# A two-layer sequence kernel: six steps take other places in their engines' queues, and nine of 128 scans run in two halves

## The reference, cut to what matters

```python
# layer 0, per batch
xn = layernorm(x) * (1 + scale) + shift            # from the condition c
x_in, z = split(xn @ in_proj_w.T)                  # 512 channels each
u = silu(causal_conv4(x_in) + conv_b)
dt_r, B, C = split(u @ x_proj_w.T)                 # 64, 16, 16 columns ("x_dbl")
dt = softplus(dt_r @ dt_proj_w.T + dt_proj_b)
# over the 256 positions, for every channel and each of 16 states:
h = h * exp(dt * A) + (dt * u) * B
y = sum over states of h * C
y = (y + u * D_param) * silu(z)
x = x + gate * (y @ out_proj_w.T)
# layer 1, per batch
q, k, v = three linear maps of layernorm(x); softmax of q over 32 features, of k over positions
y = q @ (k.T @ v); x = x + silu(layernorm(y) * (1 + s) + t) @ W_out + b_out
```

## Time and profile before

| what | value |
|---|---|
| median of three runs | 557.86 us (556.59 to 559.77) |
| the profiled execution's own time | 559.76 us |
| span of its profile | 558.0 us |
| mean granted TensorE clock | 0.887 of full speed |
| DVE scans (L1000) | 128, 291.9 us together |
| DVE multiplications by C (L1012) | 96, 117.5 us together |
| ACT decays (L766) | 512 activations, 212.7 us together |

### The profile page before, as it was taken

How to read it: one execution, slowest core, us unless ns; L and a number is a source line. 1 busy time by engine, 2 the same in 40 slices (tenths; PEclk the granted TensorE clock), 3 DMA queues, 4 the chain that set the end, 5 groups by cost and what they waited for, 6 DMA issues and landing times. The chain is left out here.

```text
span 558.0 us, 7398 instructions
## 1 busy us (share of the span) xinstructions
PE 438.2 (79%) x2438; PEld 364.5 (65%) x2438; DVE 504.7 (90%) x520; ACT 430.8 (77%) x992; POOL 449.6 (81%) x306
## 2 busy tenths in 40 slices
PE   8968756769688788779788678769677878959797
PEld 7657445557576677657676667658565766847675
DVE  2489899999999989999999999999999988999853
ACT  2694868689879989798979989799877797686444
POOL 4059979989997989979997999979997979995121
PEclk8978868887899698998899899989899697779899
DMA  8295043102330144011430044003320044000001
GB/s 250 90 330 150 0 140 97 68 23 77 120 114 2 28 153 170 3 28 52 152 122 0 29 156 168 0 11 117 122 85 9 2 165 159 1 0 20 1 1 38
DMA packets 22366, 45.38 MB, mean 81 GB/s; under 512 B 3684, under 2 KB 13556, under 8 KB 22328
## 3 DMA queue, kind: packets, MB, share of 16 engines
q1 hardware_dynamic: 22328, 44.92, 24.6%
HBM read 42.52 MB, written 2.39 MB: 80 GB/s over the span
## 5 line engine op out<-in xcount | busy, mean ns | idle before, releaser
L545 POOL TENSOR_TENSOR hs<-dtu,Br 128x1024 f32<-128x1024 f32 x127 | 296.8, 2360 | 7.9 <-DMA Br<-bc_rows 6.9
L766 ACT ACTIVATE ring<-dt,Aneg 128x256 f32<-128x256 f32 x512 | 212.7, 464 | 44.0 <-DVE hs L1012 39.1
L1000 DVE TENSOR_TENSOR_SCAN ring<-ring,hs 128x1024 f32<-128x1024 f32 x97 | 221.6, 2284 | 10.9 <-ACT ring L766 10.9
L1370 PE MATMUL sums<-ident,hs 128*128 128x128 f32 x1024 | 154.9, 309 | 49.4 <-DVE hs L1012 49.3
L1370 PEld LDWEIGHTS sums<-ident,hs 128*128 128x128 f32 x1024 | 138.6, 162 | 60.6 <-DVE hs L1012 57.5
L1012 DVE TENSOR_TENSOR hs<-ring,Cr 128x1024 f32<-128x1024 f32 x96 | 117.5, 1224 | 3.3
L554 POOL TENSOR_TENSOR hs<-hs,Cr 128x1024 f32<-128x1024 f32 x31 | 73.0, 2356 | 38.7 <-DVE hs L1000 38.7
L1000 DVE TENSOR_TENSOR_SCAN hs<-ring,hs 128x1024 f32<-128x1024 f32 x31 | 70.3, 2268 | 0.0
L1437 PE MATMUL PY<-wqkvo,xT 128*128 128x256 f32 x168 | 48.3, 439 | 0.0
L1437 PEld LDWEIGHTS PY<-wqkvo,xT 128*128 128x128 f32 x168 | 39.6, 236 | 7.7
L1363 PE MATMUL sums<-ident,uD 128*128 128x128 f32 x64 | 14.3, 310 | 32.3 <-DVE ygT L1019 32.3
(11 more groups left out here) (232 smaller groups left out, 681.7 us busy)
## 6 DMA issues: line engine op xcount, KB each, us to landing
Br<-bc_rows SPq DMA_DIRECT2D x32, 512.0 KB, 5.3
Cr<-bc_rows SPq DMA_DIRECT2D x32, 512.0 KB, 4.0
xg<-in_x SPq DMA_DIRECT2D x8, 256.0 KB, 3.0
out<-fin SPq DMA_DIRECT2D x7, 256.0 KB, 4.3
hs<-in_ada_wT SPq DMA_DIRECT2D x3, 512.0 KB, 5.1
win<-in_in_wT SPq DMA_DIRECT2D x2, 512.0 KB, 6.9
hs<-in_W_emb SPq DMA_DIRECT2D x2, 512.0 KB
gate<-gate_rows SPq DMA_DIRECT2D x8, 128.0 KB, 3.1
```

Source lines behind the costliest of these rows:

```text
L545: nc.gpsimd.tensor_tensor(hs[:, g % DBUF], dtu[:, b % 2, dc, :].unsqueeze(1).to_broadcast([P, NQ, T]), Br[:, NQ * q:NQ * q + NQ, :], ALU.m ...
L766: ins = nc.scalar.activation(ring[:, g % 2, j, :], dt[:, b % 2, dc, :], ACT.Exp, scale=Aneg[:, c:c + 1])
L1000: V.tensor_tensor_scan(driven if by_pool(g) else decays, decays, driven, 0.0, ALU.mult, ALU.add).then_inc(s_scan_done, 1)
L1370: ins = M(YT[:, c, :], hs[:, g % DBUF, j, P * c:P * c + P], ident[:, :], is_transpose=True, start=False, stop=(q == UPC - 1 and j == NQ - ...
```

## The change

Two things change.

First, the order. On ACT `copy_xdbl` goes from place 10 to 8, `softplus_parts_0` from 11 to 10 (behind `norm1`, ahead of `finish`), `softplus_parts_1` from 13 to 12. `norm1` stays in place 10. On PE `x_proj` goes from place 7 to 6 and `dt_proj_0` from 8 to 7. The lines with -6 and -5 keep the first half of dt of batch 0, which is made before the first unit, in its old turn.

Second, the scans of unit 0 and of place 8 of each batch (9 units) are done as two scans of 512 elements, two states each. The first waits for two of ACT's four decays, the second for all four. The multiplication by C stays whole, and is done by DVE in these units as before.

```diff
+def in_halves(g):
+    return g == 0 or g % U == 8
+
+def halves_until(g):
+    return sum(in_halves(i) for i in range(g + 1))
...
+        s_da_half = sem("da_half")
...
                     ins = nc.scalar.activation(ring[:, g % 2, j, :], dt[:, b % 2, dc, :], ACT.Exp,
                                                scale=Aneg[:, c:c + 1])
+                    if j == 1 and in_halves(g):
+                        ins.then_inc(s_da_half, 1)
...
-                                   (-11, copy_z), (-6, copy_xdbl), (-5, softplus_parts_0), (-3, softplus_parts_1),
-                                   (19, copy_yg), (25, normalize1), (26, norm1), (30, exp_q), (30, exp_k), (31, mask_v), (32, copy_qT),
+                                   (-11, copy_z), (-8, copy_xdbl), (26, norm1), (-6, softplus_parts_0), (-4, softplus_parts_1),
+                                   (19, copy_yg), (25, normalize1), (30, exp_q), (30, exp_k), (31, mask_v), (32, copy_qT),
...
+                    if step is softplus_parts_0 and g in (-6, -5):
+                        b = 0 if g == -5 else None
...
-                dve.wait_ge(s_da_ready, g + 1)
+                if in_halves(g):
+                    dve.wait_ge(s_da_half, halves_until(g))
+                else:
+                    dve.wait_ge(s_da_ready, g + 1)
...
+                if in_halves(g):
+                    first, second = (slice(0, 2), slice(2, NQ))
+                    for half in (first, second):
+                        if half is second:
+                            dve.wait_ge(s_da_ready, g + 1)
+                        a_half, x_half = (t[:, half].rearrange("p n t -> p (n t)") for t in (ring[:, g % 2], hs[:, g % DBUF]))
+                        ins = V.tensor_tensor_scan(a_half, a_half, x_half, 0.0, ALU.mult, ALU.add)
+                    ins.then_inc(s_scan_done, 1)
+                    dve.wait_ge(s_scan_done, g + 1)
+                    dve.wait_ge(c_loaded[q], 16 * (b + 1))
+                    V.tensor_tensor(hs[:, g % DBUF], ring[:, g % 2], Cr[:, NQ * q:NQ * q + NQ, :], ALU.mult).then_inc(s_hc_dve, 1)
+                    return
...
-                                   (-13, in_proj_3), (39, output), (-9, x_proj), (-8, dt_proj_0), (-6, dt_proj_1),
+                                   (-13, in_proj_3), (-10, x_proj), (39, output), (-9, dt_proj_0), (-6, dt_proj_1),
```

## The result

| | before | after |
|---|---|---|
| median of four runs | 557.25 us (556.59 to 559.77) | 567.95 us (567.66 to 570.46) |
| the profiled execution's own time, span | 559.76, 558.0 us | 567.85, 566.1 us |

A forecast was written before the change was run, and what follows sets the result against it. DVE was taken to set the pace, waiting 10.9 us for ACT's decays. The terms -3.72 + 0.8 + 4.97 + 4.4 = +6.45 us, put on the median 557.86, gave 564.3 us, range 559.5 to 569.5.

The forecast's parts named there:

- The halves at place 8: Place 8: split scans shorten DVE's waits for decays in batches 0 and 2 to 6, -3.72 us; eight splits cost +0.8.
- Unit 0: Start of batch 0: the split gains nothing, since scan 4 stays at about 51.0 behind the load of x.
- Softplus ahead of decays 11: Place 11: ACT's chain becomes 7.39 us against DVE's 5.85; new waits 8.76, old 3.79 gone, +4.97 us.
- The wait for `x_proj`: Between decays 8 and 9, batches 1 to 6: ACT's copy waits for PE, partly at low clock, +4.4 us.
- `softplus_parts_1` at place 12 costs nothing: DVE has `max_qk`: Place 12: the moved step costs 0, as DVE has `max_qk` and two scans before it asks for decays 13.
- rival C: PE's clock stays down as long as before: +12 us, 569.8 us, chance 0.14.
- the two terms of the order: Softplus ahead of decays 11 at place 11, +4.97 us, and ACT's wait for `x_proj` behind decays 8, +4.4.
- Rival A: PE's clock is up at `x_proj` in all batches: +2.65 us, 560.5 us, chance 0.17.
- B: The new order removes the waits at place 11 altogether: -6.7 us, 551.2 us, chance 0.05.
- D: The order does nothing, softplus displacing only ACT's idle time; only the halves count: -2.9 us, 555.0 us, chance 0.04.

The follow-up runs named there:

- e2: The kernel before with the nine split scans and nothing moved: 557.73 us, 1.000 times before.
- e6: The changed kernel with 28 small matmuls, read by nothing, in PE's queue at place 5: 564.05 us, 1.010 times before.
- e1: The changed kernel with no scan in halves, only the six steps moved: 569.55 us, 1.023 times before.
- e3: The changed kernel with both softplus steps back in places 11 and 13, behind decays 11 and 13: 558.69 us, 1.003 times before.
- e7: e3 with 28 small matmuls, read by nothing, in PE's queue at place 5: 553.74 us, 0.991 times before.
- e5: The changed kernel with the second softplus step alone back in place 13: 566.42 us, 1.017 times before.
- e11: e7 with all scans whole: 558.46 us, 1.000 times before.
- e10: e2 with 28 small matmuls in PE's queue at place 5: 552.70 us, 0.992 times before.
- e12: e7 with the layer's bias work on DVE behind unit 7 instead of unit 8: 557.11 us, 0.997 times before.

## Why the prediction was right, and where it was off

**The halves at place 8.** Right in kind: -0.79 in batch 0 and -0.66 in five batches, against -0.84 and -0.575. The split costs 0.04 to 0.05 us and not 0.1: the two halves together take 2.33 to 2.35 us, the whole scan 2.30 where it follows a wait. The 148 ns from the earlier trace rows are in the busy times (2 x 1214 - 2284 = 144), but the second half begins inside the first one's end. The Trainium skill ("VectorE: DVE Perf Modes", the section on the TRN2 errata) counts about 150 cycles at 0.96 GHz for each instruction, by which an instruction more is an estimated 0.156 us; the 0.144 us agrees in busy time, and isn't what the path pays. What was wrong is that the gain goes into the sum whole. In the old order it came back at place 11 in batches 2 and 6 (e2). In the new one it counts whole where `x_proj` is in time, since the wait there is then ACT's own work behind DVE (1.44 us in e6, 1.43 in e1 with whole scans). Where `x_proj` is late, part of it came back: 0.30, 0.54 and 0.36 us in batches 3, 4 and 6.

**Unit 0.** The trace has scan 4 0.70 us earlier, the prediction had none. But the start moves by itself: scan 4 stands at 51.27 in e1, 50.43 in e3, 51.03 in e7 and 48.14 in e2, of which e3, e7 and e2 have the split. Over all traces scan 4 stands at 50.9 to 51.3 where unit 0 is whole and at 48.1 to 51.7 where it is split. Whether the split of unit 0 is worth anything wasn't isolated.

**Softplus ahead of decays 11.** The largest term held: 7.39 us against 5.85, a wait of 1.54. In batch 4 of the changed kernel the chain took 7.52 (323.42 to 330.94), and the wait is 1.44 in e6 where nothing else disturbs. The prediction had 8.76 us of new waits from it; e5 against e3 gives 7.7 on the chip, net of what e3 lost at the taps.

**The wait for `x_proj`.** +4.4 was forecast. In the profiled run places 9 to 11 added 8.31; six chains as in e6 (5 x 1.44 + 0.95 = 8.15) less the old 3.79 are 4.36 of it, so 3.95 fell to this. By batch it was not where I put it. The forecast had 1.2, 1.4, 0.2, 0.1, 0.1 and 1.4 us in batches 1 to 6; over e6's wait stand 0.2, 0.5, 0.3, 0.5, 1.6 (places 9 to 11) and 0.4, and the rest are stops too short for the list. That the sums agree is luck. Batches 4 and 5, which I had as safe, had `x_proj` at 2.70 and 3.17 us, and batches 1 and 6, which I had as slow, at 1.89. Taking the kept clock as the test, e6 is 3.9 us under the changed kernel's median. In e6 PE was busy for 3.2 us ahead of the sums, and they ran at full pace. The rule of the Trainium skill ("TensorE: Matmul & The Clock Gate", Part 1) that activity releases the throttled level agrees with this.

**What I left out.** Three things, +2.05, +1.07 and some +1.6. First, the step "`softplus_parts_1` at place 12 costs nothing: DVE has `max_qk`". In batch 0 there is no `max_qk`, just as there is no `norm1`, which that very paragraph took into account. ACT waits 3.50 us for `dt_proj_1`, which stands on PE behind two units' sums at the low clock, and decays 13 stand behind ACT. From the timelines of PE and ACT after:

```profile
79.22 3.67 PE L1399 MATMUL sums<-ident,hs 128*128 128x128 f32 x16 [6.71 <-DVE hs L1041]
82.69 1.65 PE L1371 MATMUL PX<-xdbl,wdt 97*128 97x256 f32 x4
...
84.37 0.60 ACT L718 ACTIVATE dt<-PX 128x512 f32<-128x512 f32 x1 [3.50 <-PE PX L1371]
...
86.69 3.25 ACT L776 ACTIVATE ring<-dt,Aneg 128x256 f32<-128x256 f32 x8
```

Second, in batch 0 DVE arrived at its bias work 1.4 us earlier (71.00 against 72.45, 0.8 of it by the halves), and the first of its operations on 8 elements lasted 1.62 us in place of 0.54: it ended with POOL's operation as before. So the gain of that batch was never there. Third, the stops at places 1 to 4 of batches 2 and 4, among them DVE's waits for the taps behind unit 2 (0.43 and 0.33 us). In batch 2 PE's sums of one unit, ahead of the projection that the taps wait for, took 1.86 us where they take 1.04 at the full clock. It is rival C's kind of loss at another place.

**The sum.** The trace's 8.1 us are the 6.45 of the forecast, plus the 4.7 left out, less 0.8 for the halves (-3.74 in place of -2.92), less 0.6 and 0.45 for the two terms of the order (4.36 and 3.95 in place of 4.97 and 4.4), less 0.7 at the start and 1.46 in batch 7, plus 0.9 behind the last scan. So the forecast came near by errors that cancelled in part. The remaining 2.6 us to the 10.7 of the medians come from what the difference was put on: the profiled execution before (559.76) is 2.5 us above its median, that after (567.85) isn't.

Rival A's total (560.5) and C's (569.8) enclose the result. The changed kernel's median is nearer to C, but not for C's reason alone: without the low clock (e6) it would still be 564. B is refuted by e6, D by e5.

## What to carry to other kernels

Before a step is moved ahead of work that the bounding engine waits for, sum that engine's queue from the last point where it had to wait and compare it with the time the bounding engine takes; the old place may be the one where something else covered it. And check the batches in which that cover is missing. A gain on the bounding engine counts only as far as the next wait that hangs on another engine. Here the halves alone showed no gain (1.000, e2), and with the clock kept they are the difference between 1.000 (e11) and 0.991 (e7). In the old order halves and kept clock together gave 0.992 (e10); whether that is more than the 1.000 and 0.997 of each alone would add up to is within the intervals.

## What the runs showed of the hardware

- DVE's `tensor_scalar` on 128x8 float32 in SBUF took 0.22 us with POOL idle and up to 2.39 us beside POOL's operations of 2.33 us, ending with them each time (e12; 1.62 us after, 0.54 before). DVE's scans and multiplications with `ring` in PSUM kept 2.28 and 1.22 us beside the same POOL work. The Trainium skill ("SBUF — State Buffer", "Who interferes with whom") tells of a port pair that DVE and GpSimd (POOL) take as a whole for one instruction, `tensor_scalar` among those that can; the trace agrees.
- A scan of 512 elements took 1214 ns, of 1024 elements 2284; two halves in a row cost 0.04 to 0.05 us more than the whole on the path.
- PE's sums of two units at places 5 and 6 took 2.5 to 3.7 us behind 3.6 to 4.4 us of idle time (batches 1 to 6 of the changed kernel, granted clock 0.50 to 0.75) and 1.97 us when 28 small matmuls filled most of it (batch 4 of e6, granted clock 1.00).
